# Score products of an attention kernel: two of three contractions taken as 128 + 64 rows, the 64-row ones in pairs

## What is computed

```
x   = x + tanh(g_xattn) * attention(layernorm(x), ctx)      # x 1024 x 128, ctx 6404 x 96
out = x + tanh(g_ffn)   * experts(layernorm(x))

attention: q = xn Wq + bq, k = ctx Wk + bk, v = ctx Wv + bv      # all 128 wide
           softmax(q k^T / sqrt(128)) v
experts:   8 experts 128 -> 512 -> 128 with relu, the best 2 of each token by softmax(xn Wr + br)
```

## Time and profile before

| | us |
|---|---|
| median of 3 runs (274.19 to 274.45) | 274.2 |
| the profiled execution, its own time | 274.63 |
| its span, first to last instruction | 272.8 |
| block 0 on TensorE | 18.8 to 70.9 |
| block 1 | 70.9 to 134.2 |
| block 2 | 134.2 to 191.9 |
| slot tiles and last tiles | 191.9 to 272.8 |

### The profile page before, as it was taken

One profiled execution on the slowest core, in us unless ns is written; L12 is line 12 of the kernel. 1 busy time (PEld: TensorE's weight loads), 2 busy tenths in 40 slices (PEclk: granted clock), 3 DMA queues, 4 the chain that ended last, 5 costly groups with the idle time before them and its releaser, 6 DMA issues.

```text
span 272.8 us, 5077 instructions
## 1 busy us (share of the span) xinstructions
PE 266.9 (98%) x1662; PEld 246.2 (90%) x1662; DVE 211.2 (77%) x406; ACT 187.5 (69%) x340; POOL 109.3 (40%) x144
## 2 busy tenths in 40 slices
PE   7999999999999999999999999999999999999995
PEld 7777989999999999999899999999888998999994
DVE  4888977898386897789737578877688699468895
ACT  2897665444675557566577798888556664899992
POOL 3899993555800030000001553661025444445820
PEclk9999999999999999999999999999999999999999
DMA  6700020000089100000000222335301111323412
GB/s 188 278 2 0 0 82 0 2 1 2 0 228 340 59 0 2 0 1 2 1 0 2 77 77 79 117 117 144 111 17 31 29 32 30 98 45 75 98 31 77
DMA packets 18341, 16.89 MB, mean 62 GB/s; under 512 B 2394, under 2 KB 14796, under 8 KB 18316
## 3 DMA queue, kind: packets, MB, share of 16 engines
q1 hardware_dynamic: 17228, 15.11, 18.6%
q0 software_dynamic: 640, 1.31, 1.9%
q10 hardware_dynamic: 448, 0.14, 0.2%
HBM read 13.14 MB, written 3.42 MB: 61 GB/s over the span
## 4 chain that ended last, share of the span: by engine, by line
PE 91%; DVE 4%; DMA 2%; ACT 1%; SPq 1%; issue 0%; DVEq 0%
PE ps L1476 9%; PE ps L1502 9%; PE ps L1477 9%; PE ps L1503 9%; PE ps L1504 9%; PE ps L1478 9%; PE ps L1398 7%; PE ps L1603 4%; PE ps L1589 3%; DVE pmax L1003 2%; PE ps L1669 2%; PE ps L1670 2%; PE ps L1630 2%; PE ps L1628 2%; PE ps L1671 2%; PE ps L1629 2%
## 5 line engine op out<-in xcount | busy, mean ns | idle before, releaser
L905 ACT ACTIVATE ex_hi<-ps 128x768 fp32r<-128x768 f32 (+1 forms) x78 | 56.9, 730 | 56.0 <-PE ps L1478 54.5
L1218 DVE TENSOR_TENSOR ex_lo<-ps,ex_hi 128x768 fp32r<-128x768 f32 (+1 forms) x66 | 58.5, 886 | 23.0 <-ACT ps L909 20.7
L1003 DVE TENSOR_REDUCE pmax<-ps 128x1 f32<-128x512 f32 (+2 forms) x74 | 62.4, 875 | 10.2 <-PE ps L1398 9.5
L1502 PE MATMUL ps<-ex_hi,ctx_both 128*97 128x384 f32 (+1 forms) x153 | 49.8, 325 | 0.0
L909 ACT ACTIVATE ps<-ps 128x768 f32<-128x768 f32 (+1 forms) x66 | 49.7, 753 | 0.0
L1477 PE MATMUL ps<-q_lo,ctxT_hi 96*128 96x384 f32 (+1 forms) x153 | 49.1, 321 | 0.0
L1478 PE MATMUL ps<-q_hi,ctxT_lo 96*128 96x384 f32 (+1 forms) x153 | 48.7, 318 | 0.0
L1503 PE MATMUL ps<-ex_hi,ctx_both 128*96 128x384 f32 (+1 forms) x153 | 48.6, 318 | 0.0
L1504 PE MATMUL ps<-ex_lo,ctx_both 128*97 128x384 f32 (+1 forms) x153 | 48.6, 318 | 0.0
L1476 PE MATMUL ps<-q_hi,ctxT_hi 97*128 97x384 f32 (+1 forms) x126 | 42.3, 336 | 0.3 <-DVE ex_lo L1218 0.2
L608 POOL TENSOR_TENSOR rstd<-veps,minus_half 128x3 f32<-128x3 f32 (+1 forms) x6 | 5.0, 830 | 75.0 <-DVE veps L990 74.9
(11 more groups left out here) (231 smaller groups left out, 548.5 us busy)
## 6 DMA issues: line engine op xcount, KB each, us to landing
raw<-in_ctx_dram SPq DMA_DIRECT2D x6, 384.0 KB, 6.5
w_raw<-in_L_ffn_W_dram SPq DMA_DIRECT2D x8, 256.0 KB, 3.9
raw<-in_L_ffn_W_dram SPq DMA_DIRECT2D x8, 256.0 KB, 6.2
raw<-in_L_ffn_b_dram SPq DMA_DIRECT2D x8, 256.0 KB
shared<-routing SPq DMA_DIRECT2D x7, 192.0 KB
x_slots<-shared SPq DMA_DIRECT2D x1, 1088.0 KB, 6.3
y_slots<-shared SPq DMA_DIRECT2D x17, 64.0 KB, 1.5
shared<-in_L_ffn_b_dram SPq DMA_DIRECT2D x1, 512.0 KB, 4.0
```

Of the source, the lines that this page charges most:

```text
L905: nc.scalar.activation(ex_pair(ex_hi, u % P_RING, js, n), scores, ACT.Exp)
L1003: nc.vector.tensor_reduce(pmax[:, FIRST_TILE[ROUND_BLOCK[r]] + t, place:place + 1], max_home(s)[:, 0:w], AX.X, ALU.max).then_inc(max_reduc ...
L1218: nc.vector.tensor_tensor(ex_pair(ex_lo, u % P_RING, js, n), whole, ex_pair(ex_hi, u % P_RING, js, n).bitcast(F32), ALU.subtract).then_inc ...
L1502: nc.tensor.matmul(dst[0:CA, :], ch[:, j, :], hi, start=(j == first), stop=False)
```

## The change

Block 0 keeps its products. In blocks 1 and 2 `scores` calls `scores_later`. The 96 + 96 rows of the second and third product are cut as 128 + 64: rows 64 to 95 of the hi keys are copied under the lo keys (`ctxT_lo[96:128]`), and q_hi[0:96] with q_lo[64:96] below it is a new moving operand (`q_mixed`), which lives in `xT` or `norm`. The third product is keys' hi x q_lo over rows 0 to 63. For the second chunk of a unit (chunk number odd), rows 0 to 63 of keys and of q_lo are copied to partitions 64 to 127 (`odd_keys` in `shared`, `q_odd`), so that its 64-row product uses the other half of the array's rows; this is done for units 0 to 23 of block 2 and, since `shared` is free only after block 0, for units 6 to 23 of block 1. Elsewhere both 64-row products use the lower half. The six products of a unit are issued as hi, hi, 128-row, 128-row, 64-row, 64-row.

The copies are DMAs on SyncE. As `shared` is now taken until the last score, `bias_2` is loaded after it, the zero tile and `first_proj` move elsewhere, and the slot ring begins with `norm`. Names ending in `_r` are the same memory seen as fp32r.

```diff
+HALF = P // 2
+PAIRED_FROM = 6
...
-        first_proj = shared[:, E * P:E * P + N0 * (HID + 1)].rearrange("p (t h) -> p t h", h=HID + 1)
+        first_proj = before_lo[:, 0:N0 * (HID + 1)].rearrange("p (t h) -> p t h", h=HID + 1)
...
+        PAIRS = 6 * BANK // P
+        odd_keys = shared_r[HALF:P, :]
...
-        XS = ([x_spare[:, r, :] for r in range(X_SPARE)] + [norm[:, t, :] for t in range(PLACED)]
-              + [xT[:, t * P:(t + 1) * P] for t in range(PLACED)])
+        XS = ([norm[:, t, :] for t in range(PLACED)] + [xT[:, t * P:(t + 1) * P] for t in range(PLACED)]
+              + [x_spare[:, r, :] for r in range(X_SPARE)])
...
+        def q_mixed(b):
+            return (xT_r if b == 1 else norm_flat)[:, span(b)]
+
+        def q_odd(b):
+            return (norm_flat if b == 1 else xT_r)[HALF:P, span(b)]
...
+            sync.wait_ge(ctxT_hi_ready, NW)
+            sync.dma_start(ctxT_lo[C:P, :].bitcast(F32), ctxT_hi[HALF:C, :].bitcast(F32)).then_inc(keys_moved, 16)
+            for b in range(1, NB):
+                sync.wait_ge(q_lo_ready, b + 1)
+                sync.dma_start(q_mixed(b)[0:C, :].bitcast(F32), q_hi[0:C, span(b)].bitcast(F32)).then_inc(q_moved[b - 1], 16)
+                sync.dma_start(q_mixed(b)[C:P, :].bitcast(F32), q_lo[HALF:C, span(b)].bitcast(F32)).then_inc(q_moved[b - 1], 16)
+                sync.dma_start(q_odd(b).bitcast(F32), q_lo[0:HALF, span(b)].bitcast(F32)).then_inc(q_moved[b - 1], 16)
             sync.wait_ge(ctxT_lo_ready, TURNED_BY_VECTOR)
-            sync.dma_start(bias_2[:, :], b2.rearrange("(a e) d -> a (e d)", a=1).partition_broadcast(P).rearrange(
-                "p a n -> p (a n)")).then_inc(bias_2_in, 16)
+            sync.wait_ge(pool_lo_ready, len(POOL_LO))
+            sync.dma_start(odd_keys.bitcast(F32).rearrange("p (i k) -> p i k", k=P), ctxT_hi[0:HALF, 0:2 * PAIRS * P].bitcast(F32).rearrange(
+                "p (i two k) -> p i two k", two=2, k=P)[:, :, 1, :]).then_inc(pairs_moved, 16)
...
                 if j >= X_RING:
                     sync.wait_ge(xs_turned, j - X_RING + 1)
+                if j == X_RING - X_SPARE:
+
+                    sync.wait_ge(scores_ready, NB * UNITS)
+                    sync.dma_start(bias_2[:, :], b2.rearrange("(a e) d -> a (e d)", a=1).partition_broadcast(P).rearrange(
+                        "p a n -> p (a n)")).then_inc(bias_2_in, 16)
...
+                if b:
+                    scores_later(b, i).then_inc(scores_ready, 1)
+                    return
...
+            def scores_later(b, i):
+                js = unit_chunks(i)
+                dst = unit_scores(b * UNITS + i, js)
+                if i == 0:
+                    pe.wait_ge(keys_moved, 16)
+                    pe.wait_ge(q_moved[b - 1], 3 * 16)
+                for k, j in enumerate(js):
+                    nc.tensor.matmul(dst[:, k, :], ctxT_hi[0:CA, j * P:(j + 1) * P], q_hi[:, span(b)], start=True, stop=False)
+                for k, j in enumerate(js):
+                    nc.tensor.matmul(dst[:, k, :], ctxT_lo[:, j * P:(j + 1) * P], q_mixed(b), start=False, stop=False)
+
+                for k, j in enumerate(js):
+                    if k and j // 2 < PAIRS and (b > 1 or i >= PAIRED_FROM):
+                        pe.wait_ge(pairs_moved, 16)
+                        last = nc.tensor.matmul(dst[:, k, :], odd_keys[:, j // 2 * P:(j // 2 + 1) * P], q_odd(b), start=False, stop=True)
+                    else:
+                        last = nc.tensor.matmul(dst[:, k, :], ctxT_hi[0:HALF, j * P:(j + 1) * P], q_lo[0:HALF, span(b)],
+                                                start=False, stop=True)
+                return last
```

More of the change, by code:

```diff
@@ L174, in sb, with sb_shared @@
             return stack.enter_context(nc.sbuf_tensor(name, shape, dt))
+        def sb_shared(name, shape):
+            with nc.sbuf_tensor(name, shape, F32) as plain:
+                pass
+            return plain, sb(name + "_r", shape, F32R)
         def sem(name):
@@ L227, in attention_experts @@
         tok = sb("tok", [P, NT, D])
-        norm = sb("norm", [P, NT, D])
+        norm, norm_r = sb_shared("norm", [P, NT, D])
         stats = sb("stats", [P, 2, NT, 6])
@@ L233, in attention_experts @@
         lean = sb("lean", [P, NT])
-        xT = sb("xT", [P, NTOK])
+        xT, xT_r = sb_shared("xT", [P, NTOK])
         q_hi = sb("q_hi", [CA, NTOK], F32R)
@@ L245, in attention_experts @@
         gsum = sb("gsum", [P, NT])
-        xT_hi = sb("xT_hi", [P, SPAN], F32R)
-        xT_lo = sb("xT_lo", [P, SPAN], F32R)
+        before_hi, xT_hi = sb_shared("xT_hi", [P, SPAN])
+        before_lo, xT_lo = sb_shared("xT_lo", [P, SPAN])
         lg = sb("lg", [P, NT, E])
@@ L261, in attention_experts @@
         rT = sb("rT", [E, SPAN])
-        shared = sb("shared", [P, 6 * BANK])
+        shared, shared_r = sb_shared("shared", [P, 6 * BANK])
         acc = shared[:, 0:SPAN]
@@ L268, in attention_experts @@
         N0 = BLOCK_TILES[0]
-        first_proj = shared[:, E * P:E * P + N0 * (HID + 1)].rearrange("p (t h) -> p t h", h=HID + 1)
-        first_share = shared[:, E * P + N0 * (HID + 1):E * P + N0 * (HID + 2)]
+        first_proj = before_lo[:, 0:N0 * (HID + 1)].rearrange("p (t h) -> p t h", h=HID + 1)
+        first_share = before_lo[:, N0 * (HID + 1):N0 * (HID + 2)]
+        PAIRS = 6 * BANK // P
+        odd_keys = shared_r[HALF:P, :]
         X_SPARE, Y_RING = 3, 3
@@ L274, in attention_experts @@
         assert 5 * SPAN + (X_SPARE + 2 * Y_RING) * P <= 6 * BANK
-        XS = ([x_spare[:, r, :] for r in range(X_SPARE)] + [norm[:, t, :] for t in range(PLACED)]
-              + [xT[:, t * P:(t + 1) * P] for t in range(PLACED)])
+        XS = ([norm[:, t, :] for t in range(PLACED)] + [xT[:, t * P:(t + 1) * P] for t in range(PLACED)]
+              + [x_spare[:, r, :] for r in range(X_SPARE)])
         X_RING = len(XS)
         result = norm
+        CREST = P - C
+        norm_flat = norm_r[:, :, :].rearrange("p t d -> p (t d)")
+        def q_mixed(b):
+            return (xT_r if b == 1 else norm_flat)[:, span(b)]
+        def q_odd(b):
+            return (norm_flat if b == 1 else xT_r)[HALF:P, span(b)]
         ctxT_f = [w_raw[:, r, k, :] for r in range(W_RING) for k in range(2)] + [shared[:, k * BANK:(k + 1) * BANK] for k in range(6)]
@@ L369, in attention_experts @@
         dve_step = sem("dve_step")
+        keys_moved, pairs_moved = sem("keys_moved"), sem("pairs_moved")
+        q_moved = [sem(f"q_moved{b}") for b in range(1, NB)]
         def width(b):
@@ L523, in _ @@
             sync.dma_start(rows[E * HC:NROW, :], b2).then_inc(w_consts_in, 16)
+            sync.wait_ge(ctxT_hi_ready, NW)
[5 more added lines that the diff above has]
+                sync.dma_start(q_odd(b).bitcast(F32), q_lo[0:HALF, span(b)].bitcast(F32)).then_inc(q_moved[b - 1], 16)
             sync.wait_ge(ctxT_lo_ready, TURNED_BY_VECTOR)
-            sync.dma_start(bias_2[:, :], b2.rearrange("(a e) d -> a (e d)", a=1).partition_broadcast(P).rearrange(
-                "p a n -> p (a n)")).then_inc(bias_2_in, 16)
+            sync.wait_ge(pool_lo_ready, len(POOL_LO))
+            sync.dma_start(odd_keys.bitcast(F32).rearrange("p (i k) -> p i k", k=P), ctxT_hi[0:HALF, 0:2 * PAIRS * P].bitcast(F32).rearrange(
+                "p (i two k) -> p i two k", two=2, k=P)[:, :, 1, :]).then_inc(pairs_moved, 16)
             sync.wait_ge(slots_zeroed, 1)
             sync.dma_start(x_slots.rearrange("(j p) d -> p j d", p=P),
-                           x_spare[:, 0, :].unsqueeze(1).to_broadcast([P, SLOT_TILES, P])).then_inc(zeroes_in, 16)
+                           before_hi[:, 0:P].unsqueeze(1).to_broadcast([P, SLOT_TILES, P])).then_inc(zeroes_in, 16)
             for e in range(E):
@@ L696, in _ @@
             pool.wait_ge(ctxT_lo_ready, TURNED_BY_VECTOR)
-            nc.gpsimd.memset(x_spare[:, 0, :], 0.0).then_inc(slots_zeroed, 1)
+            nc.gpsimd.memset(before_hi[:, 0:P], 0.0).then_inc(slots_zeroed, 1)
             inverse_deviation(NB)
```

## The result

The changed kernel takes 285.5 us (median of 4 runs, 285.43 to 285.77) against 274.3 us for the kernel before on the same chip (median of 4 runs, 274.19 to 274.83): ratio 1.041, 95% interval 1.039 to 1.042, so 11.2 us slower.

What follows compares the result with a forecast made beforehand. TensorE was taken to bound blocks 1 and 2; shape changes in each unit, less 0.067 us per pair, summed to 16.9 us on the earlier kernel's 274.2, forecast as 291.0 us, range 284 to 295 us.

Steps and rivals of the forecast that it cites:

- rival B: Paired units: drain as forecast, but both halves load and run wholly in parallel, 286.5 us; chance 0.20.
- TensorE's pitch is the time of blocks 1 and 2: Blocks 1 and 2: each nanosecond TensorE gains or loses per unit reaches the kernel's end; 0.176 us per 384-column product.
- The shape change costs about 0.37 to 0.40 us out and back: Each unit of blocks 1 and 2: 0.197 us into the half-row shape, 0.173 (block 2) or 0.201 (block 1) back.
- What the pair gives back: 42 paired units: second half-row product starts 0.109 us after the first instead of 0.176, saving 0.067 us.
- Edits costed at nothing: Key, q and pair copies with their waits, later bias_2 load, moved first_proj and slot ring: all hidden, no cost.
- A: Half-row products of blocks 1 and 2: no pause, loads run ahead, each pair saves 0.138 us, 268.4 us; chance 0.10.
- C: Paired units: the two halves don't overlap at all, 19.7 us extra, 293.9 us; chance 0.20.
- D: Shape changes: only one direction is paid, the load back to the whole array runs ahead, 281.2 us; chance 0.07.
- E: Moved copies: pair rows or bias_2 land late and add a few us, 295 us and over; chance 0.04.

Runs made afterwards that it cites:

- doubling the visits: Against the kernel with both 64-row products in the lower half, each stands right behind its chunk's 128-row product, four shape changes a unit: 312.33 us, ratio 1.140.
- 65-row run: Against the changed kernel, the third score product of blocks 1 and 2 takes 65 rows, both chunks in the lower part, no pair: 274.37 us, ratio 1.000.
- kernel without pairs: Against the changed kernel, the second 64-row product of every unit uses the lower half too, as the first does: 292.71 us, ratio 1.067.

## Why the prediction was right, point by point

Slower was forecast and measured, for the reason given: each unit pays for leaving the whole array and for coming back. The number is another matter. The sum gave 291.0 us, 5.5 too many, and 285.5 lies in the range because the range was drawn around rival B as well: the range was right, not the sum. One term was wrong, what a pair gives back; the rest of the difference comes from small waits that were put at nothing.

**TensorE's pitch is the time of blocks 1 and 2.** Right for losses: the two loops got 10.8 us longer, and so did the span. For gains it holds only in part (263.35 us without the 64-row products instead of 256.4). The reading of the earlier trace rows was too narrow: it lists the waits of the products. On the load side of the same trace blocks 1 and 2 have 1.2 us more in five waits, shown below under the rest.

**The shape change costs about 0.37 to 0.40 us out and back.** Right. Forecast 0.197 in and 0.201 back (block 1), measured 0.392 for both by doubling the visits. The first six, unpaired units of block 1 took 0.37 us more on average, forecast 0.398, and unit 24 of block 2 took 0.36 more, forecast 0.37. The reading came from one maximum row, one transpose and one set of tiny products, and the 65-row run, set against the one without pairs, shows that the shape and nothing else was behind it. The drain on a change of tiling mode that the prediction cites from the Trainium skill, "TensorEngine Tiling (Array Packing)", Key Properties, agrees: in every one of the 52 units the load of L1540 isn't ahead but stands behind the 0.25 us gap.

**What the pair gives back.** This term was mis-sized: 0.067 us a pair by the load spacing of the earlier trace rows, measured 0.172, the bound that I had kept as rival B. The rows that I took it from are loads into the same rows of the array, each of which follows the one before by 0.11 (so do the 64-row loads into one half in the kernel without pairs); loads into different halves start together. A paired unit of block 2 went from 2.11 to 2.30 us, not 2.41. 42 x 0.109 = 4.6 us of the 5.6 us between 291.1 and 285.5. What the Trainium skill says in "TensorEngine Tiling (Array Packing)", Key Properties, cited beside rival B, that different tiles can load and multiply in parallel, holds here with both starts at 163.02.

**The rest, about 1 us.** Rival B's sum gave 286.5. Block 1 came to 6.66 (the sum's terms with whole pairs: 2.39 + 18 x 0.222 + 0.57 = 6.96), block 2 to 4.14 (5.4, of which some 0.3 falls behind the start of the last score product). In block 2 most units got 0.17 to 0.20 longer, against 0.194 expected, but seven (1, 2, 3, 5, 6, 11 and 15) only 0.04 to 0.12, together 0.9 less. The load side's waits of the kernel before in block 2, five in all, stand just there:

```profile
PEld ps L1476 <- DVE ex_lo L1218: 0.8, 3, 0.3
PEld ps L1551 <- DVE both L1141: 0.2, 1, 0.2
PEld ps L1514 <- ACT u_sb L853: 0.2, 1, 0.2
```

The three of L1476 are at the starts of units 2, 6 and 15: a late start lengthens the unit before, and the load that then stands beside its product (0.11) the unit itself. The other two stand behind the scores of units 11 and 3. Unit 2 shows how it looks. Before the change its first product came late, with its load beside it, 0.30 after the one ahead, and the next 0.28 later:

```profile
139.66 0.33 PE L1504 MATMUL ps<-ex_lo,ctx_both 128*97 128x384 f32 x1
139.96 0.45 PE L1476 MATMUL ps<-q_hi,ctxT_hi 97*128 97x384 f32 x1
140.24 0.34 PE L1477 MATMUL ps<-q_lo,ctxT_hi 96*128 96x384 f32 x1
...
139.96 0.19 PEld L1476 LDWEIGHTS ps<-q_hi,ctxT_hi 97*128 97x128 f32 x1 [0.31 <-DVE ex_lo L1218]
```

After the change the same unit's products stand 0.18 apart:

```profile
146.74 0.51 PE L1531 MATMUL ps<-q_hi,ctxT_hi 97*128 97x384 f32 x2
```

With longer units VectorE's subtraction is there in time: after the change no L1531 of block 2 waits for it, and about 0.12 us a unit is given back. I had put these small waits at nothing, because the earlier trace rows shows the waits of the products, and these stand ahead of the loads.

**Edits costed at nothing.** Right, by the 65-row run at ratio 1.000. The key copy (816 KB) took 5.8 us and the pair copy 6.5 us to land, and bias_2 was issued at 202.92, 4.1 us from landing, with its first use at 211.71:

```profile
ctxT_lo<-ctxT_hi SPq DMA_DIRECT2D x1, 816.0 KB, 5.8
shared_r<-ctxT_hi SPq DMA_DIRECT2D x1, 768.0 KB, 6.5
...
202.92 0.33 SPq L604 DMA_DIRECT2D shared<-in_L_ffn_b_dram  x1
...
211.71 0.46 POOL L782 TENSOR_TENSOR shared<-shared 128x128 f32<-128x128 f32 x1 [0.19 <-POOL shared L781]
```

**Rivals.** A (no pause) fell by the trace and by the 65-row run. B's mechanism is what happened. C (no overlap) fell by the run without pairs, D (one direction only) by the rows at 163.39 and by 0.392, E by the 65-row run.

## What to carry to other kernels

Two products in the two halves of the array cost one, with their loads, but going into that shape and back costs some 0.39 us, more than two 384-column products. By these numbers (0.392 / 0.172, an estimate for fp32r and 384 columns, the only case measured) pairing pays from the third pair saved per visit on, or when nothing else in the loop needs the whole array. Before splitting a contraction, look in the trace for any product of 64 rows or fewer among larger ones and read the gap on both sides; 65 rows cost what 128 do. Read the waits of the weight loads together with those of the products. And a gain on the engine that is always busy can be smaller than the same loss: here 102 products fewer gave 10.9 of 17.9 us.

## What was not expected of the hardware

Weight loads of 128 columns into the two halves started together (both at 163.02) and took 0.18 us each, no longer than one load alone (0.19 in the earlier trace rows), where loads into the same rows keep 0.11 us between them. So within the half shape two loads and two products of 384 columns fit into 0.175 us, also five times in a row.
